# DRAM scratch laid out by pairs and by groups of four graphs in a two-layer graph kernel

## What is computed

```python
h = jnp.maximum(_layernorm(x, axis=-1), 0.0)
x = x + _L0_gnn_ref(h, adj, adj, Wq, Wk, Wv, Wo)      # softmax(q k * scale + adj + adj) v, then Wo
h = jnp.maximum(_layernorm(x, axis=-1), 0.0)
# layer 1
top1 = argmax(h.mean(axis=1) @ router_w + router_b)   # one expert per graph
out = adj @ (h @ expert_w[top1])
y = (out - mean[top1]) * inv_std[top1] * gamma[top1] + beta[top1]   # mean, variance over the expert's graphs
x = x + relu(y)
```

## Time and profile before

| | us |
|---|---|
| median of 3 runs | 1491.23 |
| the three runs | 1496.55, 1491.23, 1490.86 |
| span of the profiled execution, first to last instruction | 1496.3 |

### The profile page before, as it was taken

How to read it: one execution, slowest core, us unless ns; L and a number is a source line. 1 busy time by engine, 2 the same in 40 slices (tenths; PEclk the granted TensorE clock), 3 DMA queues, 4 the chain that set the end, 5 groups by cost and what they waited for, 6 DMA issues and landing times. The chain is left out here.

```text
span 1496.3 us, 38706 instructions
## 1 busy us (share of the span) xinstructions
PE 1416.9 (95%) x11154; PEld 1255.7 (84%) x11155; DVE 1138.0 (76%) x2689; ACT 1013.9 (68%) x3145; POOL 446.1 (30%) x528
## 2 busy tenths in 40 slices
PE   7899999999999999999999999999869999999886
PEld 6898899999999999999998999899647777777765
DVE  4777887878778877787887778787766777777676
ACT  4676777777777777777777777777645555554487
POOL 0222233333233322323232332222323444444100
PEclk9999999999999999999999999999879999999999
DMA  5966555666655566666556666654524322221897
GB/s 184 261 147 148 140 130 138 155 158 158 158 140 130 132 155 155 161 154 151 130 130 147 155 161 152 156 137 117 148 79 134 129 92 88 70 86 50 308 385 292
DMA packets 141802, 228.28 MB, mean 153 GB/s; under 512 B 18356, under 2 KB 34740, under 8 KB 141748
## 3 DMA queue, kind: packets, MB, share of 16 engines
q1 hardware_dynamic: 133300, 210.86, 54.6%
q10 hardware_dynamic: 8448, 16.78, 3.0%
HBM read 88.10 MB, written 38.80 MB: 85 GB/s over the span
## 5 line engine op out<-in xcount | busy, mean ns | idle before, releaser
L269 POOL TENSOR_TENSOR prob<-prob,norm 128x512 f32<-128x512 f32 x256 | 266.7, 1042 | 743.0 <-DVE norm L373 743.0
L302 ACT ACTIVATE prob<-logits,neg_max 128x128 f32<-128x128 f32 x1024 | 398.2, 393 | 85.4 <-DVE neg_max L362 85.4
L43 PE MATMUL bank<-hT_hi,w_hi 128*128 128x256 f32 x1024 | 302.2, 295 | 7.9 <-ACT v L326 5.5
L43 PE MATMUL bank<-hT_hi,w_lo 128*128 128x256 f32 x1024 | 291.6, 285 | 0.0
L43 PE MATMUL bank<-hT_lo,w_hi 128*128 128x256 f32 x1024 | 291.0, 284 | 0.0
L357 DVE SCALAR_TENSOR_TENSOR logits<-scores_ps,adj 128x512 f32<-128x512 f32 x256 | 176.7, 690 | 103.1 <-PE scores_ps L421 99.4
L309 ACT ACTIVATE probT<-probT_ps 128x512 f32<-128x512 f32 x256 | 153.1, 598 | 102.2 <-PE probT_ps L428 97.8
L43 PEld LDWEIGHTS bank<-hT_hi,w_hi 128*128 128x128 f32 x1024 | 197.8, 193 | 16.9 <-ACT v L326 8.1
L43 PEld LDWEIGHTS bank<-hT_lo,w_hi 128*128 128x128 f32 x1024 | 197.8, 193 | 0.0
L43 PEld LDWEIGHTS bank<-hT_hi,w_lo 128*128 128x128 f32 x1024 | 197.2, 193 | 0.0
L302 ACT ACTIVATION_READ_ACCUMULATOR prob<-logits,neg_max 128x1 f32 x1024 | 194.8, 190 | 0.0
(11 more groups left out here) (133 smaller groups left out, 2805.7 us busy)
## 6 DMA issues: line engine op xcount, KB each, us to landing
stack<-qk SPq DMA_DIRECT2D x768, 128.0 KB, 2.6
x_in<-in_x SPq DMA_DIRECT2D x32, 512.0 KB, 4.7
x_res<-in_x SPq DMA_DIRECT2D x64, 256.0 KB, 2.9
x_dram<-x_res SPq DMA_DIRECT2D x64, 256.0 KB, 2.6
x_in<-x_dram SPq DMA_DIRECT2D x32, 512.0 KB, 3.7
y<-outs ACTq DMA_DIRECT2D x16, 1024.0 KB, 10.2
w_hi<-x_dram SPq DMA_DIRECT2D x7, 1024.0 KB, 12.4
out_dram<-outs SPq DMA_DIRECT2D x20, 256.0 KB, 2.1
```

Source lines behind the costliest of these rows:

```text
L43: last = nc.tensor.matmul(out, a, b, start=(n == 0), stop=(n == len(terms) - 1))
L269: nc.gpsimd.tensor_tensor(prob[:, slot], prob[:, slot], norm[:, slot].unsqueeze(2).to_broadcast([N, R, N]), ALU.mult).then_inc(normed, 1)
L302: last = nc.scalar.activation(prob[:, slot, r], logits[:, slot, r], ACT.Exp, bias=neg_max[:, slot, r:r + 1], accum_out=row_sum[:, slot, r: ...
```

## The change

`x1_dram` becomes `[B/2, N, 2, D]` (pair, node, graph in the pair, feature) and `out_dram` becomes `[B/4, N, 4, D]`. The stores still write one graph each, 2 KB for a partition, now 4 KB apart (x1) or 8 KB apart (results) in DRAM. The loads read the two graphs of a pair as one run of 4 KB for each partition, and the four results of a group as one run of 8 KB. Waits, order, number and size of the transfers stay as they are.

```diff
 # attention_layer, tokens F and Y
-sp.dma_start(x1_in[:, 2 * place:2 * place + 2], x1_dram[2 * place:2 * place + 2].rearrange("g n f -> n g f"))
+sp.dma_start(x1_in[:, 2 * place:2 * place + 2], x1_dram[place:place + 1].rearrange("p n g f -> n (p g) f"))
-sp.dma_start(x1_dram[bass.ds(2 * j + g, 1)].rearrange("g n f -> n (g f)"), x_res[:, g, :])
+sp.dma_start(x1_dram[bass.ds(j, 1), :, g].rearrange("p n f -> n (p f)"), x_res[:, g, :])
 # expert_layer, tokens X and P
-sp.dma_start(x1_in[:, 2 * g:2 * g + 2], x1_dram[bass.ds(G * group + 2 * g, 2)].rearrange("g n f -> n g f"))
+sp.dma_start(x1_in[:, 2 * g:2 * g + 2], x1_dram[bass.ds(2 * group + g, 1)].rearrange("p n g f -> n (p g) f"))
-sp.dma_start(out_dram[bass.ds(G * group + g, 1)].rearrange("g n f -> n (g f)"), out_of(group, g, False))
+sp.dma_start(out_dram[bass.ds(group, 1), :, g].rearrange("q n f -> n (q f)"), out_of(group, g, False))
 # load_x1, load_out
-sp.dma_start(x1_places[q % X1_PLACES], x1_dram[G * ORDER[q]:G * ORDER[q] + G].rearrange("g n f -> n g f"))
+sp.dma_start(x1_places[q % X1_PLACES].rearrange("n (p g) f -> n p g f", p=2), x1_dram[2 * ORDER[q]:2 * ORDER[q] + 2].rearrange("p n g f -> n p g f"))
-sp.dma_start(place_of(q), out_dram[G * ORDER[q]:G * ORDER[q] + G].rearrange("g n f -> n g f"))
+sp.dma_start(place_of(q), out_dram[ORDER[q]])
 # program
-x1_dram = nc.dram_tensor("x1_dram", [B, N, D], F32, kind="Internal").ap()
-out_dram = nc.dram_tensor("out_dram", [B, N, D], F32, kind="Internal").ap()
+x1_dram = nc.dram_tensor("x1_dram", [B // 2, N, 2, D], F32, kind="Internal").ap()
+out_dram = nc.dram_tensor("out_dram", [B // 4, N, 4, D], F32, kind="Internal").ap()
```

More of the change, by code:

```diff
@@ L228, in body @@
                             sp.wait_ge(h_transposed, 2 * PAIRS)
-                            sp.dma_start(x1_in[:, 2 * place:2 * place + 2], x1_dram[2 * place:2 * place + 2].rearrange("g n f -> n g f")).then_inc(x1_loaded[place], 16)
+                            sp.dma_start(x1_in[:, 2 * place:2 * place + 2], x1_dram[place:place + 1].rearrange("p n g f -> n (p g) f")).then_inc(x1_loaded[place], 16)
                     elif token == "W":
@@ L243, in body @@
                         wait(sp, x1_ready, 2 * j + g + 1)
-                        sp.dma_start(x1_dram[bass.ds(2 * j + g, 1)].rearrange("g n f -> n (g f)"), x_res[:, g, :]).then_inc(x1_stored[g], 16)
+                        sp.dma_start(x1_dram[bass.ds(j, 1), :, g].rearrange("p n f -> n (p f)"), x_res[:, g, :]).then_inc(x1_stored[g], 16)
                     elif token == "K":
@@ L487, in expert_layer @@
     ew_hi, w_raw, w_raw_loaded, ew_hi_ready, ew_split, x1_in, x1_loaded = shared
-    B, N, D = x1_dram.shape
+    B, N, D = y.shape
     E = w_raw.shape[1]
@@ L653, in body @@
                         wait(sp, h2_ready, G * (group - 1) + 2 * g + 2)
-                        sp.dma_start(x1_in[:, 2 * g:2 * g + 2], x1_dram[bass.ds(G * group + 2 * g, 2)].rearrange("g n f -> n g f")).then_inc(x1_loaded[g], 16)
+                        sp.dma_start(x1_in[:, 2 * g:2 * g + 2], x1_dram[bass.ds(2 * group + g, 1)].rearrange("p n g f -> n (p g) f")).then_inc(x1_loaded[g], 16)
                     elif token == "J":
@@ L662, in body @@
                         wait(sp, out_copied, G * group + g + 1)
-                        sp.dma_start(out_dram[bass.ds(G * group + g, 1)].rearrange("g n f -> n (g f)"), out_of(group, g, False)).then_inc(out_stored[g], 16)
+                        sp.dma_start(out_dram[bass.ds(group, 1), :, g].rearrange("q n f -> n (q f)"), out_of(group, g, False)).then_inc(out_stored[g], 16)
             run(sp, body)
@@ L669, in load_x1 @@
                 if q != LAST:
-                    sp.dma_start(x1_places[q % X1_PLACES], x1_dram[G * ORDER[q]:G * ORDER[q] + G].rearrange("g n f -> n g f")).then_inc(x1_chunk_loaded[q], 16)
+                    sp.dma_start(x1_places[q % X1_PLACES].rearrange("n (p g) f -> n p g f", p=2), x1_dram[2 * ORDER[q]:2 * ORDER[q] + 2].rearrange("p n g f -> n p g f")).then_inc(x1_chunk_loaded[q], 16)
             def load_out(q):
                 sp.wait_ge(y_stored[q - STAYED], 16)
-                sp.dma_start(place_of(q), out_dram[G * ORDER[q]:G * ORDER[q] + G].rearrange("g n f -> n g f")).then_inc(out_chunk_loaded[q - STAYED], 16)
+                sp.dma_start(place_of(q), out_dram[ORDER[q]]).then_inc(out_chunk_loaded[q - STAYED], 16)
             sp.wait_ge(z_made, B)
```

## The result

The changed kernel is slower.

| runs of the changed kernel | its median, us | the kernel before beside it, us | ratio, 95% interval |
|---|---|---|---|
| the change as it stands | 1505.08 | 1492.09 | 1.0083 [1.0063, 1.0102] |
| again, on another chip (after_again) | 1506.74 | 1497.29 | 1.0072 [1.0053, 1.0092] |
| a third time (after_third) | 1501.78 | 1497.26 | 1.0047 [1.0028, 1.0066] |

The account below looks back on a forecast made before the run. PE was taken to bound attention and the expert stage, no full engine the last stage, where graphs pass between PE, ACT and DVE. All terms were 0: profiled span 1496.3 us unchanged, 5.1 above the median, so about 1491; range 1484 to 1498.

Parts of the forecast that it names:

- Longer reads: Expert and last stage loads: 9856 fewer packets save 2.0 and 2.9 us per DMA engine, off the path; term 0.
- y beside longer packets: Last stage: load packets may push y back and delay load_out, harmless within 15.2 us of slack; term 0.
- Stores with gaps: Attention: x1 and result stores land as today; term 0, last x1 store -0.6 to +4.0 us.
- The doubt raised from the Trainium skill: Stores: row pitch at a large power of two may halve their rate, adding 0.7 us to the last one: 1491.9.
- The faster one: Last stage: full DMA engines slow it in ways waits don't show; relief gives 1477 to about 1484.5 us; chance 0.10.
- The slower one: Attention, Z0's wait at line 241: gapped stores landing after about 12 us bound SP; 13 us gives about 1517; chance 0.08.

Follow-up runs that it names:

- doubled stores: Kernel before with every x1 stored twice in attention: both contiguous, 1574.25 us, ratio 1.0549; both 4 KB apart, later reads in 2 KB runs, 1571.8 us, 1.0528.
- pool_after: Changed kernel, but in the last stage POOL loads the expert number and copies its coefficients ahead for ACT and DVE: 1486.23 us, 0.9965 of the kernel before.

## Why the prediction was wrong

*Longer reads* held as far as it went: 9856 packets gone, DMA share down by 4 points, the loads off the path. (Its "16 fewer packets per engine and load" in the expert stage should be 128 / 16 = 8; the 0.06 us beside it is worked out from 8.)

*y beside longer packets, term 0, is the step that failed.* It asked the right question, what happens if longer load packets push y back, and named one way to the end: `load_out` starts later, by more than 15.2 us. That way stayed closed. The wait at line 674 grew by 5.0 us, and the loads landed sooner. What counted was the reverse: the loads were done 9 us earlier, and y, pushed back, went out alone at full rate for 14 us longer. In that time the register loads of lines 762 and 880 take 637 ns in place of 301. About ten graphs (14 us at the stage's 1.4 us each) with 0.34 us more are 3.4 us; the chain has 4.4 us more on line 762, ACT's loads took 4.6 us more in sum, and the stage took some 4 us more over the kernels with long reads of both tensors (90.8 to 92.8 us) than over those with 2 KB reads of both (86.8 to 88.6). The term should have been about +4. That is a third to somewhat over half of the 7 to 12 us; the rest lies in no stage that the profiles agree on.

Behind it lies a reading. The prediction looked for transfers among the releasers and found none, before and after, rightly. It took this for proof that transfers don't matter. They do matter by slowing instructions that wait for nothing. The chain's "ACTq L762" was on the page before the change, at 1% of the whole span, 15% of the last stage; a look at its loads, 274 ns at least and 870 at most before the change, would have shown a duration on the path that something trebles.

*Stores with gaps, term 0.* The bounds of -0.6 to +4.0 us were for the last store alone. It did as forecast: 1.7 us again. For the rest, "even a landing of 6.6 us is covered" rested on K0, which DVE's `qk` holds for 9.6 us. The doubled stores show the cover is not whole: ACT waits behind Y1', X and K1' too. What the gaps add is between 0 and 7 us and not settled, in size or in place; a price of 0 is not shown either.

*The doubt raised from the Trainium skill* (DMA: Bandwidth & Descriptors, Latency and other measured facts), that rows at large powers of two apart may store more slowly, does not show at 4 KB: the x1 stores land in a median of 2.7 us, before 2.6. At 8 KB something like it may: the 20 result stores land in a median of 2.5 to 2.7 us in the seven profiles with that pitch and of 2.0 to 2.2 in the others, most of the 0.7 us that the prediction reckoned for a halved rate. Nothing waits for them, and whether the power of two or the gap as such does it, no run shows.

*The rivals.* The faster one falls: with less DMA work the stage grew. Its premise, that full engines slow the stage in a way that the waits don't show, is what the runs found, with the opposite sign. The slower one named the wrong place: its sign was right, but line 241's wait is 119.4 us, far below the 400 that it asked for. And the base was low: 1491.23 was a median of three, and later comparisons on other chips gave 1491.3 to 1499.9 for the same kernel. This doesn't touch the sign, which was found within each chip.

## What to carry to other kernels

Where two queues share the DMA engines, making one queue's packets longer can give it the time of the other, as here from 2 KB to 4 and 8 KB; ask what the pushed-back queue will then run beside, not only whether somebody waits for it. A list of releasers shows who waits for whom, but not who is slowed by whom: look in the chain for sequencer entries (ACTq, DVEq) and at the spread of their durations. And test a cause by a sum that must stay the same: here the stage less ACT's register loads. A register load per tile belongs on an engine with time to spare, ahead of its use: here that was worth 0.6% with the old layout, more than either layout alone.

## What was not expected of the hardware

A register load from SBUF took some 272 ns at its least and over 1 us at its most (1047 and 1073 ns after the change), and its median doubled while y was read from SBUF at over 320 GB/s. POOL's loads slowed as well, with no other load of that tensor beside them (median 953 ns in pool_after). With 1 KB load packets beside y it slowed at about half that rate of y (405 ns, 17 loads). The Trainium skill (DMA: Bandwidth & Descriptors, Latency and other measured facts) gives some 600 ns as the floor of such a load; the least and the median here are half of that, so the measurement decides, and 600 ns is what it takes beside a full y. Packets of 2, 4 and 8 KB took 84, 159 and 309 ns (medians of the last stage's traces), so the fixed part is some 9 ns, near the 8 that the earlier trace rows gave.
